# First attention layer: the row maxima stored head by query tile, and turned with one transpose of 16 columns per group of heads

## The reference

```
q  = layer_norm(transpose(x   + pos))          # per batch: 512 tokens x 256
kv = layer_norm(transpose(ctx + pos))
Q, K, V = q @ Wq, kv @ Wk, kv @ Wv             # 16 heads of 16
attn = softmax(Q K^T / 4) V                    # per head 512 x 512 scores
r = attn @ Wo + q
out = gelu(layer_norm(r) @ W1 + b1) @ W2 + b2 + r
```

## Time and profile before

| | |
|---|---|
| three runs | 1864.43, 1862.97, 1859.38 us |
| span of the profiled execution | 1856.0 us (first to last instruction; the profile gives no device time of its own for it) |
| busy share of the span: TensorE matmul, weight load, VectorE, ScalarE, GpSimd | 94%, 67%, 66%, 58%, 5% |
| mean granted TensorE clock | 0.965 of full speed |
| first layer: a round of one batch, 156 us to 563 us | 81.3 us each |
| in such a round: TensorE busy | 79.8 us |
| chain that ended last | TensorE 81%, VectorE 9%, ScalarE 5% |

### The profile page before, as it was taken

One profiled execution on the slowest core, in us unless ns is written; L12 is line 12 of the kernel. 1 busy time (PEld: TensorE's weight loads), 2 busy tenths in 40 slices (PEclk: granted clock), 3 DMA queues, 4 the chain that ended last, 5 costly groups with the idle time before them and its releaser, 6 DMA issues.

```text
span 1856.0 us, 34276 instructions
## 1 busy us (share of the span) xinstructions
PE 1736.2 (94%) x12832; PEld 1244.6 (67%) x12832; DVE 1216.0 (66%) x2792; ACT 1071.9 (58%) x2333; POOL 99.5 (5%) x79
## 2 busy tenths in 40 slices
PE   4879999999999988999999989999999889999999
PEld 2324343444434333788888878888888779999998
DVE  5666776767776552488887887888887753333332
ACT  2346666756666574587778777777777731111111
POOL 1110101101000000000000000000000000000000
PEclk7779999999999898999999999999999999999999
DMA  6322223222222222566656766666665340000000
GB/s 160 120 82 61 91 85 97 69 92 89 81 70 66 80 61 85 140 160 167 173 149 177 196 170 189 175 174 174 172 166 154 114 144 23 23 24 23 26 28 16
DMA packets 168334, 201.73 MB, mean 109 GB/s; under 512 B 25573, under 2 KB 115813, under 8 KB 168169
## 3 DMA queue, kind: packets, MB, share of 16 engines
q1 hardware_dynamic: 167880, 199.14, 38.2%
q10 hardware_dynamic: 288, 0.39, 0.1%
HBM read 131.84 MB, written 67.63 MB: 107 GB/s over the span
## 4 chain that ended last, share of the span: by engine, by line
PE 81%; DVE 9%; ACT 5%; issue 2%; DMA 1%; DVEq 1%; ACTq 0%; SPq 0%; POOL 0%
PE c_d L2099 10%; PE c_sums L2114 9%; PE b_d L1361 9%; PE b_d L1373 9%; PE a_d L501 6%; PE b_d L1440 5%; PE a_escore L472 5%; PE a_d L579 3%; PE a_d L571 3%; PE a_mscore L484 3%; PE b_score L1428 3%; PE a_d L555 3%; PE b_d L1457 3%; DVE a_mx L804 2%; PE a_d L563 2%
## 5 line engine op out<-in xcount | busy, mean ns | idle before, releaser
L804 DVE TENSOR_REDUCE a_mx<-a_mscore 128x2 f32<-128x1024 f32 x247 | 301.9, 1222 | 170.6 <-PE a_mscore L484 169.2
L641 ACT ACTIVATE a_pt<-a_escore 128x1024 f32<-128x1024 f32 x256 | 262.5, 1025 | 164.2 <-PE a_escore L472 163.7
L1590 ACT ACTIVATE b_pr<-b_t,b_nmax 128x256 f32<-128x256 f32 x512 | 254.4, 501 | 124.7 <-DVE b_nmax L1766 124.7
L1762 DVE TENSOR_TENSOR b_t<-b_score,b_mask 128x1024 f32<-128x1024 f32 x128 | 155.1, 1212 | 85.6 <-PE b_score L1428 85.2
L2198 ACT ACTIVATE c_gT<-c_d,c_b 128x256 f32<-128x256 f32 x128 | 53.7, 472 | 267.4 <-PE c_d L2099 267.4
L1766 DVE CUSTOM_DVE_ANT_0 b_t<-b_t,b_minus 128x256 f32<-128x256 f32 x512 | 187.5, 422 | 16.8
L472 PEld LDWEIGHTS a_escore<-a_qst,a_kst 50*128 50x128 f32 x512 | 49.9, 191 | 180.7 <-ACT a_pt L641 106.1
L472 PE MATMUL a_escore<-a_qst,a_kst 50*128 50x512 f32 x512 | 133.2, 516 | 24.9 <-ACT a_pt L641 23.9
L2243 DVE CAST c_g_high<-c_gT 128x512 fp32r<-128x512 f32 x64 | 40.2, 629 | 172.0 <-ACT c_gT L2198 172.0
L2099 PE MATMUL c_d<-c_ln_high,c_w_high 128*128 128x256 f32 x512 | 144.7, 283 | 2.3 <-DVE c_ln_low L2245 2.3
L2099 PE MATMUL c_d<-c_ln_high,c_w_low 128*128 128x256 f32 x512 | 144.9, 283 | 0.0
(11 more groups left out here) (165 smaller groups left out, 3271.3 us busy)
## 6 DMA issues: line engine op xcount, KB each, us to landing
b_qst<-b_q SPq DMA_DIRECT2D x96, 256.0 KB, 4.8
b_kst<-b_k SPq DMA_DIRECT2D x96, 256.0 KB, 6.4
b_q<-b_qparts SPq DMA_DIRECT2D x64, 256.0 KB, 4.5
b_k<-b_kparts SPq DMA_DIRECT2D x64, 256.0 KB, 3.4
a_qst<-a_q_parts SPq DMA_DIRECT2D x192, 64.0 KB, 2.2
a_kst<-a_k_parts SPq DMA_DIRECT2D x186, 64.0 KB, 2.2
a_k_parts<-a_kparts SPq DMA_DIRECT2D x32, 256.0 KB, 2.3
a_q_parts<-a_qparts SPq DMA_DIRECT2D x32, 256.0 KB, 2.3
```

The lines of the kernel that those rows point to most:

```text
L641: nc.scalar.activation(pt[:, at % RING, :, :], escore[:], ACT.Exp, scale=SCALE).then_inc(exp_done.sem, 1)
L804: nc.vector.tensor_reduce(mx[:, q, 2 * pair:2 * pair + 2], maxima_bank(b, n)[:], AX_X, ALU.max).then_inc(max_done.sem, 1)
L1590: last = nc.scalar.activation(pr[:, u % 2, j, :], t[:, u % 2, j, :], ACT.Exp, scale=-1.0, bias=nmax[:, u, j:j + 1], accum_out=esum[:, u, j ...
```

## The change

`mx` is stored as heads by query tiles instead of query tiles by heads, so that the 16 maxima of one group (4 heads x 4 tiles) lie in 16 adjacent columns. They are turned with one transpose, which leaves 16 partitions (head, tile) of 128 queries in the PSUM bank. `mparts` has the same shape, and so the copies of ScalarE and VectorE read 16 x 128 instead of 4 x 512. The DMA into the scratch writes the same 16 KB to the same addresses, from 16 partitions. What reads the scratch is the same.

```diff
-        mx = sb("mx", [P, TT, HEADS])
-        mparts = sb("mparts", [GROUP, 2, T], F32R)
+        mx = sb("mx", [P, HEADS, TT])
+        mparts = sb("mparts", [TT * GROUP, 2, P], F32R)
...
-                sp.dma_start(scratch_m[b].rearrange("t h n -> h t n")[heads], mparts[:].bitcast(F32)).then_inc(m_out.sem, 16)
+                sp.dma_start(scratch_m[b][:, heads, :].rearrange("a h (t n) -> (h t) a n", n=P), mparts[:].bitcast(F32)).then_inc(m_out.sem, 16)
...
-                for t in range(TT):
-                    last = nc.tensor.transpose(at[0:GROUP, t * P:(t + 1) * P], mx[:, t, g * GROUP:(g + 1) * GROUP], ident[:])
-                last.then_inc(m_filled.sem, 1)
+                nc.tensor.transpose(at[0:TT * GROUP, 0:P], mx[:, g * GROUP:(g + 1) * GROUP, :].rearrange("p h t -> p (h t)"), ident[:]).then_inc(m_filled.sem, 1)
...
-                nc.scalar.activation(mparts[:, 0, :], bank("m", b, g)[0:GROUP, :], ACT.Copy, scale=-1.0).then_inc(m_high.sem, 1)
+                nc.scalar.activation(mparts[:, 0, :], bank("m", b, g)[0:TT * GROUP, 0:P], ACT.Copy, scale=-1.0).then_inc(m_high.sem, 1)
...
-                nc.vector.tensor_reduce(mx[:, q, 2 * pair:2 * pair + 2], maxima_bank(b, n)[:], AX_X, ALU.max).then_inc(max_done.sem, 1)
+                nc.vector.tensor_reduce(mx[:, 2 * pair:2 * pair + 2, q], maxima_bank(b, n)[:], AX_X, ALU.max).then_inc(max_done.sem, 1)
...
-                nc.vector.scalar_tensor_tensor(mparts[:, 1, :], bank("m", b, g)[0:GROUP, :], -1.0, mparts[:, 0, :].bitcast(F32),
+                nc.vector.scalar_tensor_tensor(mparts[:, 1, :], bank("m", b, g)[0:TT * GROUP, 0:P], -1.0, mparts[:, 0, :].bitcast(F32),
```

## The result

The changed kernel takes 1847.41 us (median of four runs, 1846.49 to 1848.91), the kernel before 1863.7 us (median of four, 1859.38 to 1864.87). The ratio is 0.992, with an interval of 0.9904 to 0.9936: 12 to 18 us faster. 1852.2 us was forecast, with a range of 1847.0 to 1859.5 us.

A forecast was written before the change was run, and what follows sets the result against it. TensorE, busy 79.8 of 81.3 us per round, was taken as the bound. Terms 7.6 + 2.4 + 1.0 - 0.2 = 10.8 us took the span from 1856.0 to 1845.2 us, median 1852.2 us, range 1847 to 1859.5 us.

The forecast's parts named there:

- The counted terms: Turns at full and half clock plus helper copies on the chain, less weight load: 10.8 us gain, bounds 6.9 to 11.6.
- changes of clock at the start: Slow start of the first layer: three changes of clock saved would bring the time to 1847 us.
- Three transposes of 0.109 us per turn: TensorE's queue, four transposes become one: 0.33 us less per turn at full clock, 7.6 us over 23 turns.
- The 0.20 us that remain: Of a turn's 0.53 us on the chain, the way into and out of the array, paid once with either number.
- The weight load: TensorE's load grows from 4 to 16 columns: about 5 ns more per turn, 0.2 us in all.
- The short copies: ScalarE's high part 0.23 us, VectorE's low part about 0.30 us; mostly idle time, 1.0 us on the chain.
- position 4: VectorE runs without a gap there; without a shorter low part about 7 of 32 turns bring nothing, 2.3 us less gain.
- The turns at half clock: Five on the chain, the first counted at nothing; four save 0.59 us each, 2.4 us.
- Behind the first layer: Everything there moves earlier as a whole; waits hang only on semaphores of earlier work, so nothing is taken back.
- The clock row: Granted clock of the whole span: three slices at 7, one at 8 around 640 us, nearly all else at 9.
- The base: Median of the runs taken as 7.0 us above the profiled span of 1856.0 us, the same distance assumed after.
- Rival 3: Shorter turns make the clock fall at two waiting places per round: 20 us cost less 10.8 gain, 1872 us; chance 0.04.

The follow-up runs named there:

- e5: The kernel before run again with no edit; 1864.15 us (ten runs).
- e2: Changed kernel with its transpose issued four times into the same place, copies still 16 x 128; 1860.17 us, ratio 0.9984.
- e3: Changed kernel with one transpose, but ScalarE's and VectorE's copies both lengthened to 16 x 512; 1853.85 us, ratio 0.9954.
- e12: Changed kernel with its transpose issued seven times (six more); 1860.41 us, one execution.
- e7: Changed kernel with 16 extra transposes at one place in the second layer; 1851.53 us.
- e10: Changed kernel with the DMA write of the maxima done three times, each waited for; 1849.19 us, one execution.
- e11: Changed kernel with the DMA write of the maxima done seven times, each waited for; 1871.67 us, one execution.
- e4: Changed kernel with one transpose, ScalarE's copy short (16 x 128), only VectorE's copy long (16 x 512); 1853.41 us, ratio 0.9951.
- e8: Changed kernel with 32 extra transposes at one place in the second layer; 1856.14 us.

## Why the prediction was right, and where it was not

The change acts where and as the prediction said, in the rounds. That the median of the runs fell into the range was luck in part. The counted terms gave 6.9 to 11.6 us, and 16.3 us came between the medians. The range reached down to 1847 us only for changes of clock at the start, and those gave nothing. What filled it was a change of clock 1200 us later, which the prediction did not have in its sum.

The spans of the profiled executions, cut at the same marks (us): the start of the first high part at full clock, of the one five rounds later, of the last high part, of the last `b_rstd` and of the `c_res` sum, and the end.

| | before | changed | e5 (before) | e2 | e3 | e12 |
|---|---|---|---|---|---|---|
| to the first mark | 156.7 | 157.4 | 157.8 | 155.2 | 155.2 | 150.7 |
| five rounds | 406.8 | 400.4 | 406.8 | 406.9 | 400.6 | 413.4 |
| rest of the first layer | 121.4 | 120.2 | 121.4 | 120.7 | 120.8 | 123.2 |
| to the last `b_rstd` | 681.4 | 679.3 | 681.5 | 678.8 | 678.7 | 680.4 |
| to `c_res` | 169.6 | 169.7 | 175.8 | 175.7 | 176.0 | 171.3 |
| to the end | 320.2 | 320.2 | 320.2 | 320.2 | 320.2 | 319.6 |

- **Three transposes of 0.109 us per turn: right.** 0.33 us forecast, 0.32 us measured between before and after, 0.109 us per transpose by e2 and e12. Over the 20 turns at full clock 6.6 us was forecast, 6.4 us came. The 0.20 us that remain came out as 0.21 us.
- **The weight load: right**, 3 ns against 5 ns.
- **The short copies:** forecast 0.23 and 0.30 us, measured 0.25 and 0.27 us. That they are worth nothing in a settled round was right by e2 and e3. That position 4 would have kept its old time without them was wrong: the place was read correctly, but the next wait behind it, on ScalarE's `hT`, has 0.7 us to give and hides it. I had followed the chain for one step and not for two.
- **The turns at half clock: the mis-sized term.** 2.4 us were forecast. The chain shows 0.63 us less for each, but between 563 us and the last turn the gain is 1.2 us where the terms give 2.2: the intervals of the high part show 0.61 us won at the turn near 642 us (17.81 to 17.20 us) and 0.81 us lost in the next (21.44 to 22.25 us). The half clock lasted longer there: about 10.2 us from 635 us on before, 13.6 us from 626 us on in the changed kernel. The 1.2 us are not of the queue alone: one transpose with long copies (e3) gives 0.65 us of them, four with short copies (e2) 0.7 us. The time to the first mark scatters by 2 us within either kernel (156.1 to 157.8 us before, 155.1 to 157.6 us after) and shows no gain that can be told.
- **Behind the first layer: not nothing.** From the last high part to 1366 us the changed kernel needs 679.3 us, the one before 681.4 us. About 0.35 us is the short high part on the path to the Gelu (forecast); the rest lies in half-clock stretches and in a wait for a transfer between 690 and 755 us. e2 and e3 have it too (678.8 and 678.7 us), so neither the number of transposes nor the length of the copies decides it. What separates these kernels from the one before in this point was not settled.
- **The clock row: misread.** The earlier trace rows have a second slice at 8, that from 696 to 742 us, where the prediction counted one. It lies in the time in which the 2 us behind the first layer were won.
- **The base: wrong.** I put the median 7.0 us above the span and took that as what lies around it. It is 1.8 us, within 0.1, in all runs. The other 5.2 us were the distance from a profiled execution of the lower heap to a median in the upper. Taken from span to span the forecast was -10.8 us and the trace shows -8.9 us, with 1 us of scatter from the start in each.
- **The 6 us beside the change.** Over all 62 runs of the kernel before (e5's ten with them), 13 lie below 1860 us, 49 above. All ten runs of the changed kernel lie at 1846 to 1849 us, and all profiled executions of it and of its edits e7, e10 and e11 pass the stretch in 169.6 to 169.8 us. e5 and the changed kernel differ by 16.3 us in span, just as the medians do. By the table that is 6.4 us in the five rounds, which e2 and e12 show to be the transposes; 1.2 us in the rest of the first layer; 2.2 us behind it, not settled; 6.1 us in the stretch where the clock fell in e5 and not in the changed kernel; and 0.4 us at the start, which is scatter. Rival 3 had such a fall of the clock in the wrong place and with the wrong sign: not in the rounds of the first layer, where the clock stayed at 1.00, but 700 us later, and in favour of the change. The prediction had put this at nothing, with the sentence that all behind the first layer moves earlier as a whole. The reason why the changed kernel's timing falls on the good side is not shown; e3 and e4, with nearly the same rounds and the same TensorE queue, fall on the bad one.

## What to carry to other kernels

When a small gain is sized, compare marks inside the traces (here the starts of one copy, which repeat to 0.05 us over five rounds), not only the end: the end carried 6 us of clock from a stretch that no edit had touched, and they made the change look larger and e3 and e4 look like losses. On an engine that is busy for 98% of a round, what leaves its queue comes off the round at the spacing of its neighbours in the stream (0.109 us), not at its own duration (0.27 us). Before a wait elsewhere is priced, look at the wait that follows it: 0.7 us of idle time right behind hides what is lost ahead.

## What the runs showed of the hardware

- The same program with the same wait of TensorE (1.11 of 3 us busy) was followed by 1.00 in one execution and by 0.50 in another. The time of the whole stretch from the last `b_rstd` to `c_res` was 169.6 to 169.8 us in six profiled executions, 175.7 to 176.1 us in six, and 172.9 (e8) and 171.3 us (e12) in one each.
- A float32 transpose with a stationary operand of 16 columns costs the stream as much as one with 4: with four of each, rounds of 81.38 and 81.35 us. Packing more columns into one transpose was free.
- Copies out of PSUM follow the columns, not the partitions: 16 x 512 (e3) took ScalarE 0.57 us and VectorE 0.67 us, as 4 x 512 did before; 16 x 128 took 0.25 and 0.27 us.
- The same 16 KB written to DRAM from 16 partitions in pieces of 512 bytes landed sooner than from 4 partitions in pieces of 2 KB: 1.42 us against 1.72 us from the issue of the write to that of the read which waits for it (medians of 32 in the first execution of each).
